# Softmax sums of an attention kernel: from ScalarE's second exponential pass to GpSimd adds and a matmul by ones

## The reference

```python
x = x + attention(layernorm(x), ctx, ctx, mask, Wq, bq, ...)   # 16 heads of 32
#   sim = q @ k.T * scale; attn = softmax(sim); out = attn @ v; out @ Wo + bo
x = x + moe(layernorm(x), Ws, bs, W1, b1, W2, b2)
#   probs = softmax(x @ Ws + bs) over 8 experts; each expert takes its 512 best
#   of 4096 tokens, gelu(xin @ W1 + b1) @ W2 + b2, times its prob, added back
```

## Time and profile before

| | us |
|---|---|
| median of 3 runs | 1845.64 (1834.13 to 1846.29) |
| the profiled execution | 1831.13 |
| its span, first to last instruction | 1829.2 |

### The profile page before, as it was taken

How to read it: one execution, slowest core, us unless ns; L and a number is a source line. 1 busy time by engine, 2 the same in 40 slices (tenths; PEclk the granted TensorE clock), 3 DMA queues, 4 the chain that set the end, 5 groups by cost and what they waited for, 6 DMA issues and landing times.

```text
span 1829.2 us, 21959 instructions
## 1 busy us (share of the span) xinstructions
PE 1621.5 (89%) x7667; PEld 1158.9 (63%) x7667; DVE 1111.6 (61%) x1950; ACT 987.3 (54%) x2111; POOL 357.9 (20%) x505
## 2 busy tenths in 40 slices
PE   4779979799799898897998639999999999999997
PEld 3546646456456465464664328778888888888885
DVE  5675766766757757667675456777545555554543
ACT  3788778787777877887878402222223223232322
POOL 4122221231221322312312111010202020201101
PEclk9789989999899899898998859999999999999998
DMA  6344452634453536435435122242525252525231
GB/s 213 111 126 137 144 155 80 214 110 137 126 150 130 153 92 186 122 116 169 143 113 165 70 70 93 70 140 97 167 70 167 70 167 69 168 73 180 83 108 23
DMA packets 127653, 227.46 MB, mean 124 GB/s; under 512 B 17852, under 2 KB 52304, under 8 KB 127544
## 3 DMA queue, kind: packets, MB, share of 16 engines
q1 hardware_dynamic: 98168, 142.55, 24.1%
q0 software_dynamic: 29376, 83.52, 16.4%
HBM read 166.36 MB, written 59.13 MB: 123 GB/s over the span
## 4 chain that ended last, share of the span: by engine, by line
PE 73%; DMA 9%; DVE 6%; ACT 5%; issue 4%; POOL 1%; SPq 0%; POOLq 0%; ACTq 0%; DVEq 0%
PE ps_gen L677 8%; PE ps_gen L679 8%; PE ps_gen L678 8%; PE ps_gen L1718 6%; PE ps_gen L1720 6%; PE ps_gen L1719 6%; PE ps_att L1576 6%; PE ps_gen L1545 6%; PE ps_gen L1565 4%; PE ps_gen L1531 3%; DMA qst<-qk_rows 3%; PE ps_gen L1532 2%; PE ps_gen L1533 2%; DMA x_in<-in_ctx 2%; ACT ps_gen L999 2%
## 5 line engine op out<-in xcount | busy, mean ns | idle before, releaser
L1176 DVE TENSOR_REDUCE nmax<-ps_gen 128x1 f32<-128x512 f32 x512 | 340.5, 684 | 96.9 <-PE ps_gen L1545 95.4
L999 ACT ACTIVATE ps_gen<-ps_gen,nmax 128x512 f32<-128x512 f32 x512 | 342.0, 671 | 86.8 <-DVE nmax L1176 85.0
L1011 ACT ACTIVATE p_ring<-ps_gen,keep_scale 128x512 f32<-128x512 f32 x512 | 338.1, 690 | 82.3 <-PE ps_gen L1565 82.1
L1061 ACT ACTIVATE gel<-ps_gen,b_cols 128x512 f32<-128x512 f32 x128 | 88.3, 690 | 451.0 <-PE ps_gen L679 450.9
L1545 PE MATMUL ps_gen<-kst,qst 97*128 97x512 f32 x512 | 232.0, 470 | 58.3 <-issue 37.2
L1430 DVE TENSOR_TENSOR gel_lo<-gel,gel_hi 128x512 fp32r<-128x512 f32 x126 | 87.3, 693 | 288.5 <-ACT gel_hi L1062 288.5
L1545 PEld LDWEIGHTS ps_gen<-kst,qst 97*128 97x128 f32 x512 | 106.6, 209 | 179.3 <-issue 122.8
L1565 PE MATMUL ps_gen<-qst,kst 99*128 99x512 f32 x512 | 200.5, 442 | 17.7 <-ACT ps_gen L999 12.9
L677 PE MATMUL ps_gen<-hT_hi,w_hi 128*128 128x512 f32 x512 | 203.2, 397 | 1.5 <-DVE hT_lo L1423 1.5
L678 PE MATMUL ps_gen<-hT_lo,w_hi 128*128 128x512 f32 x512 | 200.3, 391 | 0.0
L679 PE MATMUL ps_gen<-hT_hi,w_lo 128*128 128x512 f32 x512 | 200.3, 391 | 0.0
(11 more groups left out here) (196 smaller groups left out, 2655.3 us busy)
## 6 DMA issues: line engine op xcount, KB each, us to landing
w_raw<-in_L_ffn_W SPq DMA_DIRECT2D x128, 512.0 KB, 4.5
kst<-qk_rows POOLq DMA_DIRECT2D x96, 256.0 KB, 4.1
qst<-qk_rows SPq DMA_DIRECT2D x96, 256.0 KB, 4.0
x_in<-in_x POOLq DMA_DIRECT2D x60, 256.0 KB, 4.6
qk_rows<-kT_hi POOLq DMA_DIRECT2D x32, 256.0 KB, 2.3
qk_rows<-kT_lo POOLq DMA_DIRECT2D x32, 256.0 KB, 2.5
qk_rows<-qT_hi SPq DMA_DIRECT2D x32, 256.0 KB, 3.0
qk_rows<-qT_lo SPq DMA_DIRECT2D x32, 256.0 KB, 4.1
```

The source lines that it names most:

```text
L999: e.activation(psum[:, :], psum[:, :], ACT.Exp, bias=nmax[g % 2][:, c], scale=-1.0, accum_out=den[g % 2][:, c]).then_inc(drained_sem("max" ...
L1011: e.activation(p_ring[n % NP_][:, :], ps("score", g, kt, h)[:, :], ACT.Exp, scale=keep_scale[:, b:b + 1]).then_inc(drained_sem("score", g, ...
L1176: e.tensor_reduce(nmax[g % 2][:, h * TB + t:h * TB + t + 1], ps("max", g, h, t)[:, :], AX.X, ALU.min).then_inc(s_min, 1)
```

## The change

ACT's pass over the max banks goes, and with it `den`, `recip` of 128x16, its transpose and copy. POOL adds the four exponential tiles of each head into the first (`sum`, three adds a head, twelve a group), and for each head PE multiplies the sum tile by ones (`den`): 16 matmuls of 32 columns, where a one-hot column of `pick`, repeated every fourth, puts token tile t at each fourth row. DVE's reciprocal reads 128x128 from PSUM. The result is stored (64 KB) and loaded with repetition (`spread`, `spread_in`). `divide` comes in the next group. ACT copies `ps_att` to `att_n` (`taken`), v and the route transposes, DVE no longer. `p_ring` has ten tiles and an explicit list of free ones, `oT` half its columns, and the statistics four slots. All transfers of the loop are issued by SyncE; `keep` and `stack` come in a high and a low step. All tables of places are new, and each engine but PE sorts the steps by time plus a lag of its own.

```diff
-NP_ = 6
+NP_ = 10
+NSTAT = 4
...
+    def order_of(self, lags):
+
+        def at(n):
+            inside = 0 <= self.times[n] < NG
+            return self.times[n] + (lags.get(self.steps[n][0], 0) if inside else 0)
+        return [self.steps[n] for n in sorted(range(len(self.steps)), key=at)]
...
-            a.max_of(0, h, t)
+            a.with_bank("max", 0, h, t)
...
+    DEN_AT, SPREAD_AT, SPREAD_IN_AT, DIVIDE_AT, OSPLIT_AT = 0.14, 0.18, 0.27, 0.43, 0.41
...
+        "pool": {"sum": 0.03, "stats": -0.02, "out": -0.02, "add_bias": -0.01},
...
+                elif kind == "sum":
+                    g, kt, h = at
+                    on.wait_ge(*drained("score", g, kt, h))
+                    on.wait_ge(s_av, g * KT + 1)
...
+                    e.tensor_tensor(p_tile(g, 0, h), p_tile(g, 0, h), p_tile(g, kt, h), ALU.add).then_inc(summed(g, kt, h)[0], 1)
...
-                    e.activation(psum[:, :], psum[:, :], ACT.Exp, bias=nmax[g % 2][:, c], scale=-1.0, accum_out=den[g % 2][:, c]
-                                 ).then_inc(drained_sem("max", g, h, t), 1)
...
+                    was = agenda.p_before[g, kt, h]
+                    if was is not None:
+                        was_g, was_kt, was_h = was
+                        if was_kt == 0:
+                            on.wait_ge(*full("den", was_g))
+                        else:
+                            on.wait_ge(s_av, was_g * KT + was_kt + 1)
+                            on.wait_ge(*summed(was_g, was_kt, was_h))
...
+                    e.activation(att_n[:, :], ps_att[:, :], ACT.Copy).then_inc(s_taken, 1)
...
-                                    ).then_inc(s_min, 1)
+                                    ).then_inc(drained_sem("max", g, h, t), 1)
...
+                    on.wait_ge(*full("den", g))
...
+                    e.reciprocal(rden_b[:, 0:P], ps("den", g)[:, 0:P]).then_inc(drained_sem("den", g), 1)
...
-                    e.tensor_tensor(att_n[:, :], ps_att[:, :], rden_b[:, :], ALU.mult).then_inc(s_nrm, 1)
...
+                    on.wait_ge(s_spread_in, 16 * (g + 1))
+                    e.tensor_tensor(att_n[:, :], att_n[:, :], rden_b[:, :], ALU.mult).then_inc(s_nrm, 1)
...
+                    on.wait_ge(*summed(g, KT - 1, HG - 1))
+                    by_four = pick[:, :, :].rearrange("p a b -> p (a b)")
+                    for t in range(TB):
+                        for h in range(HG):
+                            last = e.matmul(ps("den", g)[h * DH:(h + 1) * DH, 0:P], lhsT=by_four[:, TB - 1 - t:TB - 1 - t + DH],
+                                            rhs=p_tile(g, 0, h)[:, t * P:(t + 1) * P], start=(t == 0), stop=(t == TB - 1))
```

425 lines of the change are left out of this document (222 added, 203 removed).

## The result

The changed kernel takes 1869.0 us, median of four runs (1868.5 to 1871.5); the kernel before, beside it on the same chip, 1839.9 (1825.2 to 1846.3). The ratio is 1.017, with a 95% interval of 1.010 to 1.024: slower, though whether by as much as 2% is not clear. I had predicted 1773 us, range 1726 to 1836, so the prediction was wrong, in its sign too. Two of my rivals end on this side, (d) and the second half of (c) (1879 us); I had given "slower" 11%.

The account below looks back on a forecast made before the run. PE was held by banks that ACT's second pass frees: 1831.1 us - 71.4 (seven batches) - 7.7 (last batch) - 1.0 (before the loop) + 15.1 (end) + 7.3 (toward the median) = 1773 us, range 1726 to 1836.

Parts of the forecast that it names:

- (d): DVE waits at the division for two transfers, holding minima and PE: 124 us more, 1897 us; 8%.
- (c): The fixed order, not ACT, held PE: 1853 us, or (second half, PE's share 0.812 kept) 1879 us; 8%.
- Part 5: SyncE issues about 40 more transfers a batch, at most 21 us, costed at nothing because of the lag-sorted order.
- Part 3: POOL adds 48 tiles a batch, 61.2 us, reaching 70.8 us a batch, 63% busy, hidden under PE.
- the ring's arithmetic: Ten exponential tiles hold: PE wants a group's last sums about 8 us later, against 5.1 us of POOL adds.
- the tail: After the last group, POOL's adds, sums, reciprocal and two transfers start the last division later: +15.1 us.
- Part 2: DVE loses copies and a small reciprocal, gains four 128x128 reciprocals of 0.84 us: 83.8 to 80.6 us a batch.
- rival (a): DVE's two-SBUF-input instructions and POOL lock each other out: 4.5 us a batch more on DVE, 1808 us; 10%.
- What bounds the kernel now: In the attention loop, PE's 11.2 us idle a batch before max matmuls awaits PSUM banks freed by ACT's second pass.
- Rival (b): PE in the loop gets as dense as in the experts' stage: 106.1 us a batch, 1718 us; 12%.

Follow-up runs that it names:

- a_unwaited: Changed kernel with both spread transfers issued (load 384 columns wide) but DVE's division not waiting for them, using the 128 reciprocal columns repeated: 1839.3 us.
- a_nospread: Changed kernel without the two spread transfers; DVE's division uses the 128 columns of reciprocals repeated, POOL's additions stay: 1818.1 us.
- a_memset2: Changed kernel without the spread transfers, each POOL addition replaced by three write-only memsets of about the same total length: 1791.0 us.
- a_neither: Changed kernel without POOL's additions and without the two spread transfers: 1763.8 us.
- b_noexp: Kernel before without ACT's second pass over the score tiles, every softmax sum set to the constant 512: 1822.9 us.
- c_early: Changed kernel, whole computation, with the spread's load right behind its store in SyncE's order in every group: 1843.5 us.

## Why the prediction was wrong

The account, in the order in which parts were taken out of the changed kernel. "By ratios" takes each kernel's ratio times 1839.9 us:

| step | us | by ratios | a batch | from |
|---|---|---|---|---|
| changed kernel | 1869.0 | 1871.5 | 125.7 | |
| DVE's wait for the spread | -29.7 | -33.3 | -3.5 | a_unwaited |
| the spread's bytes at that place, and the last group's wait | -21.2 | -22.1 | -1.7 | a_nospread |
| DVE and POOL blocking each other | -27.1 | -30.4 | -3.8 | a_memset2 |
| POOL's own time | -27.2 | -16.9 | -2.9 | a_neither |
| what is left | 1763.8 | 1768.9 | 113.9 | |

What is left is 76 us below the kernel before, and the forecast of 1773 was 73 below its 1845.6. The two don't mean the same, since a_neither has no additions and no transfers at its end either: from the last group's first score matmul to the end it takes 821.1 us, as before (822.1), where the forecast had 15.1 more. From the loop's first score matmul to that of the last group it is 71.5 us shorter than before, where I had 79. So nine tenths of what the loop was to gain is there. Of the 105 us that the two added parts cost, 17 are the end (838.6 against 821.1), of which I had 15.1 in the sum; the rest, costed at nothing or nearly, turned the sign.

**Part 5, SyncE: "I cost this at nothing".** This step failed most, at 51 us. I had looked at issues and not at landings. Rival (d) had the place and the queue behind it right: waits in two of four groups, not three, of 2.6 us each (31.0 us in 12), and 54.6 us over the whole program. They cost 30 us and not 124. In the groups that waited, the division started 9.6 to 10.6 us after the reciprocal's end (forecast 8.5): the load was issued 3.0 to 3.6 us after the store, since another step of SyncE stood between, and landed 6.5 to 7.0 us later. Where it was issued at once, 1.6 us after the store, the division found it landed 8.0 to 9.0 us after the reciprocal's end. That the load would also slow k's rows was in no rival.

**Part 3, POOL: "It hides under PE".** By the ring's arithmetic it did; yet its time costs 27 us (17 by the ratios) with DVE undisturbed. Part of this is the tail, which I had in the sum: the stretch from the last group's first score matmul to the end is 833.8 us in a_memset2 and 821.1 in a_neither, 12.7 apart. The rest, 2.9 us a batch, I had not: PE is idle 6.3 us a batch instead of 5.2, and busy 1.8 longer at a granted clock of 0.96 instead of 0.975. Which of POOL's dependants is late there, tiles of the ring or the sums, no run separates; in the last group both are late: the last attention matmul starts 21.4 us into it instead of 14.8, and the last sum matmuls wait 8.8 us for POOL.

**Part 2, DVE, and rival (a).** The mechanism stood in the prediction, the size was off by three: 4.5 us a batch were forecast, 92.05 - 79.45 = 12.6 came. I counted 12 instructions with two SBUF inputs, which came to 8.5 us. I left out the eight normalisations, which have one: 3.2 us more, at 976 ns each instead of 578; small additions of the router make up the rest. And I let each wait for half an addition in 59% of cases, 0.38 us, while oT_lo in a_nospread took 1778 ns, 1.01 us over its 771 in a_neither, four fifths of an addition each time. (The reciprocal of 128x128, put at 0.84 us, took 0.96, which is 0.5 us a batch.) Against my 35 us for 4.5, the 11.2 of them that a_memset2 takes away cost 27: the price per microsecond was too high by more than three, which made up for it. By the Trainium skill (SBUF — State Buffer, Who interferes with whom) a DVE instruction with two SBUF inputs is blocked by GpSimd's reads and not by its writes, and tensor_scalar in a two-port mode by either: the traces agree, with 0.75 and 1.59 us for oT_lo, and with 617 ns for the normalisation (a tensor_scalar) beside memsets, 578 beside neither and 976 beside additions. That the normalisation runs in such a mode no run here shows.

**What bounds the kernel now.** The reading of the earlier trace rows was wrong in part: of 11.2 us before the max matmuls the rows name ACT's second pass for 1.2, and the 9.7 put down to "issue" I gave to it as well. So did rival (c)'s "PE's most frequent waits are for banks which ACT gives back". b_noexp left the waits at 110.3 us. This was rival (c)'s "'issue' hides what the wait was for", and its half of the truth: the kernel before had ACT's pass and q's transfers one behind the other. Without the pass and with the maxima 0.12 of a group later, the old order came to 1808.6 us, and a_neither to 1763.8. The change also has other places for projections and maxima, issues all transfers of the loop from SyncE in lag order, and has a longer ring; no run takes these out, so which of them brings the other 45 us stays open. The gain was nearly right, its cause only in part.

**What was right.** ACT's 61.6 us; DVE's 80.6, by a_neither 79.45; the sum matmuls at 1.0 us a group, in the loop. The batch of 113.2 us, with 113.9 in a_neither, is partly luck: at a granted clock of 0.975 PE's work there is 108.7 - 0.025 x 113.9 = 105.8 us, not 103.0, and its share of the time 0.93, not 0.91, two errors that cancel. The tail at 15.1 of 16.5 us is luck too, as shown above. Rival (b), 106.1 us a batch, did not come even there.

**The chances.** (a), (c) and (d) had 26% between them, each alone. That several hold at once was not among the cases, though they don't exclude one another, and added up, at their measured sizes, they turn the sign. Of all the numbers (c)'s 126.8 us a batch and 1879 us lie nearest to the measured 125.7 and 1869, but not for its reason: the new order came to 113.9 once the two added parts were out. Two slips of working stand in the prediction: 1742 to 1803 belongs to shares of 0.944 to 0.88, while 0.95 to 0.87 gives 1736 to 1814; and the forecast and the four rivals already add up to 100%, without the 2 kept for other waits. Neither changes the outcome.

## What to carry to other kernels

Moving work to an idle engine is priced in three parts: its own time, its landings (a result that goes through DRAM costs two landings, and the queue's order can add to them), and what it does to the instructions it runs beside: here additions on POOL, busy with them for half of the time, made DVE's instructions with two SBUF inputs 0.5 to 1.0 us longer on average, and left those that read PSUM as they were. Of a wait put down to "issue", ask which transfers the waiting instruction reads before giving it to an engine. And where rivals can hold together, price them together.

## What the runs showed of the hardware

Beyond the blocking above: in the batches the load of the spread reciprocals (256 KB) landed 6.5 to 7.0 us after its issue where the division waited for it, and 6.1 to 7.0 in c_early; loads of q's rows, of the same size, had a median of 3.7. The row of the latter, from the page's DMA issues of the changed kernel (KB, median us to landing):

```profile
qst<-qk_rows SPq DMA_DIRECT2D x96, 256.0 KB, 3.7
```

In the last group, with no other transfer issued beside it, the spread's load still took 4.6 us. Two windows of the changed kernel, first while that load ran alone, then while two loads of q's rows and one of x ran (last numbers: granted clock, DMA share, GB/s):

```profile
1060.00:1062.00 2.00, 0.00 (x0) 0.00 (x0) 0.00 (x0) 0.00 (x0) 0.00 (x0) 1.00 0.26 102
```
```profile
495.00:495.50 0.50, 0.00 (x0) 0.00 (x0) 0.50 (x1) 0.00 (x0) 0.30 (x1) 0.50 0.99 377
```

The share is that of 16 engines, so the spread's load kept about four of them busy, and the other three together all of them. By the Trainium skill (DMA: Bandwidth & Descriptors, Rules for kernel authors) a transfer whose outermost size is under 16 uses at most as many DMA engines, and this one's pattern begins with the four heads, where q's begins with 32 rows. The trace agrees, with its share of 0.26; a load with another order of its sizes was not tried.

The median landing of the stores of k's low rows went from 2.0 to 3.6 us when a load of 192 KB was issued among k's stores, with that of the high rows still at 2.0. When the load went ahead of them, both were 2.7.
